# A fused attention and mixture-of-experts layer on one core: where TensorE's products of probabilities and values stand in its queue

## The reference

```python
qkv = x @ w_qkv.T                       # 16 heads of 16
q, k = rope(rms_norm(q)), rope(rms_norm(k))
attn = softmax(causal(q @ k.T) * scale) # per head, 512 x 512
out = (attn @ v) @ w_proj.T
x = layernorm(x + out)
normed = rms_norm(x) * norm_weight
top 2 of 8 experts by sigmoid(normed @ router_w.T), weights normalised
y = relu(normed @ sw1 + sb1) @ sw2 + sb2
  + sum over the chosen experts e: w_e * (relu(normed @ ew1[e] + eb1[e]) @ ew2[e] + eb2[e])
x = layernorm(x + y)
```

## Time and profile before

| | before |
|---|---|
| median of 3 runs | 952.51 us (952.02 to 952.53) |
| profiled execution | 957.52 us, span 955.8 us |
| PE busy | 896.0 us (94%) |
| ACT, DVE, POOL busy | 615.3, 576.6, 457.2 us |
| mean granted TensorE clock | 0.984 |

### The profile page before, as it was taken

The page is one execution under the profiler, slowest core; times in us unless marked ns, Lnnn a source line. Parts: engine busy times, 40 slices in busy tenths (PEclk is TensorE's granted clock), DMA queues, the critical chain, the costliest instruction groups (busy, mean ns, idle before and its releaser), DMA issues.

```text
span 955.8 us, 26112 instructions
## 1 busy us (share of the span) xinstructions
PE 896.0 (94%) x9049; PEld 693.3 (73%) x9050; DVE 576.6 (60%) x1152; ACT 615.3 (64%) x1060; POOL 457.2 (48%) x668
## 2 busy tenths in 40 slices
PE   4789999998999989999999999999999999999995
PEld 1444555555555546888889989989899889898885
DVE  8655698889888636784344444454444433428875
ACT  4788898888878766442656655556655453667753
POOL 5344557877878636572134444344434343412211
PEclk9799999999999989999999999999999999999998
DMA  5112223433212255567882122121212121248641
GB/s 175 67 68 95 94 101 106 158 114 135 101 58 84 69 176 194 202 204 266 267 292 74 50 67 70 52 68 55 67 56 67 46 68 47 74 145 269 214 160 44
DMA packets 68706, 112.76 MB, mean 118 GB/s; under 512 B 7728, under 2 KB 46000, under 8 KB 68496
## 3 DMA queue, kind: packets, MB, share of 16 engines
q1 hardware_dynamic: 51248, 77.32, 24.5%
q10 hardware_dynamic: 10896, 16.40, 5.9%
q0 software_dynamic: 6480, 17.97, 5.2%
HBM read 66.58 MB, written 45.08 MB: 117 GB/s over the span
## 4 chain that ended last, share of the span: by engine, by line
PE 76%; ACT 7%; DVE 6%; issue 4%; POOL 2%; DMA 2%; another core or an unknown queue 1%; ACTq 1%; DVEq 0%; SPq 0%; POOLq 0%
PE hb L1811 23%; PE yb L1827 23%; PE pv_bank L1599 6%; PE slot L1577 4%; PE ma L1612 4%; PE slot L1586 3%; PE hb L1665 3%; ACT prob L872 2%; PE mb L1747 2%; PE ma L1622 1%; PE tr L1685 1%; DMA rs<-resid 1%; PE yb L1702 1%; PE mb L1735 1%
## 5 line engine op out<-in xcount | busy, mean ns | idle before, releaser
L1042 ACT ACTIVATE hf<-hb,b 128x256 f32<-128x256 f32 (+1 forms) x392 | 155.0, 454 | 206.2 <-PE hb L1811 200.7
L1811 PE MATMUL hb<-xgT,wts 128*128 128x256 f16 (+1 forms) x1872 | 213.2, 263 | 1.4 <-ACT hf L1042 1.2
L1827 PE MATMUL yb<-wts,hh 128*128 x1704 | 210.5, 273 | 0.9 <-DVE hh L1454 0.9
L1454 DVE TENSOR_TENSOR hh<-hf,hh 128x1024 f16<-128x1024 f32 (+1 forms) x98 | 120.2, 1229 | 137.3 <-ACT hh L1047 105.4
L1811 PEld LDWEIGHTS hb<-xgT,wts 128*128 x1872 | 181.2, 98 | 20.3 <-ACT hf L1042 1.0
L807 POOL DMA_INDIRECT y_tok<-yb,dest x71 | 77.8, 1096 | 227.0 <-DVE yb L1466 216.9
L1827 PEld LDWEIGHTS yb<-wts,hh 128*128 128x128 f16 x1704 | 166.3, 98 | 19.6 <-DVE hh L1454 1.2
L872 ACT ACTIVATE prob<-slot 128x1024 f32<-128x1024 f32 x160 | 161.6, 1034 | 27.8 <-PE slot L1586 27.3
L1047 ACT ACTIVATE hh<-hf 128x1024 f16<-128x1024 f32 (+1 forms) x98 | 97.6, 996 | 3.1
L741 POOL DMA_INDIRECT xg_rows<-xnh,sl_i x64 | 76.4, 1194 | 16.2 <-issue 13.9
L1577 PE MATMUL slot<-stk 64*128 64x128 f16 (+3 forms) x512 | 64.2, 308 | 16.2 <-ACT prob L872 11.6
(11 more groups left out here) (236 smaller groups left out, 1445.0 us busy)
## 6 DMA issues: line engine op xcount, KB each, us to landing
wts<-in_w_all SPq DMA_DIRECT2D x23, 512.0 KB
wts<-y_tok SPq DMA_DIRECT2D x32, 256.0 KB, 4.9
xg<-xg_rows ACTq DMA_DIRECT2D x30, 264.0 KB
stage<-in_w_all SPq DMA_DIRECT2D x12, 512.0 KB
w_split<-chunk_hl SPq DMA_DIRECT2D x12, 512.0 KB
xTf<-in_xT SPq DMA_DIRECT2D x8, 512.0 KB, 3.8
xin<-in_x SPq DMA_DIRECT2D x8, 512.0 KB
resid<-y SPq DMA_DIRECT2D x16, 256.0 KB
```

The source lines that it names most:

```text
L1042: act.activation(hf[:, c, 0:size], hb[c // 2][:, (c % 2) * TT:(c % 2) * TT + size], ACT.Relu, bias=bias, scale=1.0 / WS).then_inc(S("relu_ ...
L1454: dve.tensor_tensor(hh[:, par, 1, cs, 0:size], hf[:, cs, 0:size], hh[:, par, 0, cs, 0:size], ALU.subtract).then_inc(S("h_lo"), 1)
L1811: ins = pe.matmul(hb[hc // 2][:, (hc % 2) * TT:(hc % 2) * TT + size], weights(e, c, w, hc * P, P), xgT[:, par, x * DC + c, 0:size], start= ...
L1827: ins = pe.matmul(ybank[par][:, j * D:(j + 1) * D], hh[:, par, x, hc, P * j:P * j + P], weights(e, DC + hc * D // CH, w, hc * D % CH, D), ...
```

## The change

PE's call of `attended` is moved within a position from behind the scores to behind RANK, which is behind all jobs but the early shared-expert pieces. The tables of positions, the waits, and the queues of all other engines stay as they are.

```diff
                         scores(c, p)
-                    for c, i in due(AV, g):
-                        attended(c, i)
                     for c, t in due(TR, g):
                         stacked(c, t)
...
                         last.then_inc(S("rank_done"), 1)
+                    for c, i in due(AV, g):
+                        attended(c, i)
                     for kind, m, q in early_due(g):
```

## The result

| | before | changed |
|---|---|---|
| median of 5 runs each | 952.51 us (951.89 to 953.70) | 956.66 us (956.3 to 956.9) |
| ratio | | 1.0053, 95% interval 1.0042 to 1.0064 |
| profiled execution, span | 957.52, 955.8 us | 956.66, 954.9 us |
| mean granted clock | 0.984 | 0.981 |

The change makes the kernel 4.15 us slower, 0.3 us off the forecast of 956.4. One thing in this table needs a word. So the two spans can't be subtracted, and I compare stages that lie ahead of it.

A forecast was written before the change was run, and what follows sets the result against it. PE bounds the kernel, busy 896.0 of 955.8 us. +2.15 us at full clock plus 1.7 us for one clock fall give 3.85 us, so 956.4 us against the median 952.51; range 949.5 to 961.0 us.

The forecast's parts named there:

- Position 6, the waits: TR at position 6 waits for POOL's second copy in batches 3 to 6: some 2.5, 2.5, 1.8, 1.6 us.
- What they cost at full clock: Loss left at position 6 after give-back in batches 3 to 6: 1.2, 1.2, 0 and 0.65 us.
- A place missed: Position 6 of batches 1 and 2: POOL's copies were over before AV began, so no lateness was counted.
- Position 16: ACT's exponential of unit 17 starts sooner: 0.45 us won in batches 0 and 1 each; gains of batches 2 to 5 counted nothing.
- The sum at full clock: Position 16's gains and position 6's losses over all batches: +2.15 us.
- The clock: PE's clock falls to half behind one of the four late places at position 6: 1.7 us.
- the first rival: Serving ACT earlier at position 16 wins, position 6 costs nothing: 2.85 us faster, 949.7 us; chance 0.15.
- The second: Waits at position 6 appear, but the clock holds and some position 16 gain survives: 1.0 us or less, 953.5; chance 0.17.
- The last: Half clock in each late place at position 6: 961.5 us; chance 0.13, shared with a further unseen wait.
- batch 7's gain as 0: NAT passes AV in batch 7, but DVE and ACT would meet the same stall: bounds 0 and -2.2 us, taken 0.

The follow-up runs named there:

- experiment 4: Changed kernel with POOL's scatters of tiles 1 to 3 of batches 0 to 6 moved later, against the kernel before: 954.83 us, ratio 0.9967.
- experiment 2: AV late at position 6 only, at its old place elsewhere, against the kernel before: 959.39 us, ratio 1.0009.
- experiment 1: AV late at position 16 only, at its old place elsewhere, against the kernel before: 954.98 us, ratio 0.9974.
- experiment 9: AV late at position 16 in all batches and at position 6 in batch 7 only, against the kernel before: 950.88 us, ratio 0.9990.
- experiment 10: AV late at position 6 of batches 3 and 4 only, against the kernel before: 955.49 us, ratio 1.0050.
- filled kernel: Changed kernel plus 8 useless fp32 matmuls ahead of TR at position 6, batches 3 to 6, against the kernel before: 956.17 us (0.9975), again 951.43 us (0.9994).
- experiment 5: Changed kernel run again in the second group, against the kernel before: 961.76 us, ratio 1.0046.
- experiment 12: Changed kernel run a third time, in the third group, against the kernel before: 955.81 us, ratio 1.0051.
- experiment 6: Kernel before, unchanged, run again with a profile in the second group: 957.07 us, ratio 0.9994.
- experiment 7: AV late at position 16 only and POOL's scatters late, against the kernel before: 957.56 us, ratio 1.0006.
- experiment 8: Kernel before with POOL's scatters late and nothing else, against the kernel before: 959.25 us, ratio 1.0015.

## Why the prediction was right

By its own steps, in the stage unless said:

- **Position 6, the waits.** Forecast 2.5, 2.5, 1.8, 1.6 us; measured 2.55, 2.63, 1.57, 1.56. Right in place, releaser and size. That POOL's own queue holds the copy is shown by experiment 4.
- **What they cost at full clock.** Forecast 1.2, 1.2, 0 and 0.65; experiment 2 gives 1.09, 1.02, -0.06 and 0.18. Batches 3 to 5 right, batch 6 too high by 0.5: more of the delay was given back than the two waits of PE that I counted. No run singles out where.
- **A place missed.** In batch 2 I called TR free since POOL's copy was over. But TR also waits for `ma_free`, that is for ACT's square of QK, and that costs 0.35 us of waiting. Experiment 2 has +0.40 in that batch; with the gain of position 16 beside it the changed kernel shows -0.17.
- **Position 16.** Batch 0: forecast -0.45. From the start of a score unit at 63.14 us to that of one at 79.05, the stretch that holds position 16, PE takes 15.91 us before and 15.37 in the changed kernel, -0.54. Batch 1: forecast -0.45, and -0.58 in experiment 1 (40.82 to 40.24). I counted the gains of batches 2 to 5 as swallowed. The idle 0.26 and 0.36 us of experiment 1 show the swallowing, but not all of it happens: the changed kernel still has -0.40 in batch 5 against before.
- **The sum at full clock.** Forecast +2.15. Measured: -0.52 ahead of the stage; within it 4.59 - 2 x 1.6 = +1.4; behind it -0.26 (experiment 9). Together +0.6, so this part was too high by some 1.5 us.
- **The clock.** Forecast one fall of 1.7 us, with 0 to 4 possible. The size was right: 1.58 us between experiments 10 and 2, 1.6 between the changed and the filled kernel in both batches (45.23 - 43.60, 46.22 - 44.63), and 1.60 between experiments 5 and 12 in batch 6 (43.28 - 41.68). The number was too low: two in two profiles of the changed kernel, three in the third. This part was too low by 1.5 us. That I took one fall rested on the fall behind the idle 1.96 us at 43 us, and that was one throw of several: the same wait of 1.95 or 1.96 us stands in all 14 profiles and the clock fell behind it in five, and not in the second profile of the kernel before (experiment 6).

So the forecast of +3.85 against +4.15, +4.12 and +3.92 measured is right in mechanism and sign, but its closeness is luck: two errors of 1.5 us and of opposite sign cancel. The terms that were mis-sized are the number of falls, one in place of two or three, and the sum at full clock, +2.15 in place of +0.6.

**The rivals.** The kernel of experiment 1 is what the first rival describes, and its condition, copies that come in time, doesn't hold; so the gain is 1.3 us in the stage, and with batch 0's 0.54 ahead of it some 1.9, and not 2.85. The second, in which the clock holds, is what experiment 2's profile shows, with a stage of +2.63. The last, a half clock in each late place, falls short: behind the waits of 1.56 to 1.58 us the clock held in five of six cases of the changed kernel. The Trainium skill, "TensorE: Matmul & The Clock Gate", section "HAM oscillation — how this bites in real kernels", describes a kernel whose passes each wait for input, longer than PE waits here, and each restart at the low rate. The trace agrees in batches 3 and 4 of all three profiles of the changed kernel and in batch 6 of one, and disagrees in the other five of their twelve late places.

**When does it fall?** Not by the length of the wait alone. It fell behind all six waits of 2.55 to 2.64 us for POOL in the changed kernel, behind 2.26 in experiment 10, and behind 2.51, 2.75 and 1.81 us for an exponential in experiments 4 and 7; it held behind 2.27 and 2.35 in experiment 2, behind 2.35 in experiment 10, and in experiment 8 it held behind one of 2.48 for an exponential; it fell once behind 1.57 (experiment 5). What decides it between 1.6 and 2.5 us is open.

**The stretch at 341 us.** In the first profile of before, ACT and DVE did nothing together for 4.8 us, up to 345.28 us (the prediction saw only its last 2.9). The same in experiment 6, the kernel before in the second group, timelines of ACT and DVE and the busy time:

```profile
345.64 1.02 ACT L872 ACTIVATE prob<-slot 128x1024 f32<-128x1024 f32 x1 [4.79 <-remote]
```

```profile
345.65 0.26 DVE L1190 RECIPROCAL rcp<-mb 128x16 f32<-128x16 f32 x1 [4.70 <-remote]
```

```profile
341.00:346.00 5.00, 2.44 (x32) 1.12 (x22) 0.32 (x2) 0.36 (x1) 2.78 (x3) 0.98 0.32 111
```

The first profile of the changed kernel doesn't have it:

```profile
341.00:346.00 5.00, 4.66 (x54) 2.08 (x54) 4.39 (x10) 2.83 (x4) 3.78 (x5) 1.00 0.42 149
```

It would be easy to credit the change with that. But in all eight profiles of the first two groups ACT idles 4.75 to 5.03 us ahead of one exponential between 342 and 350 us, in those with AV late in batch 7 too, and in all four of the third it idles 2.24 to 2.39 us there, in experiment 10 with AV early in batch 7 too. Between the second AVs of batches 6 and 7 the former take 36.7 to 38.6 us and the latter 33.5 to 33.7. It goes with the group and not with the queue order, nor with the chip, which is the same in the first and third group; and it is of the size by which the medians of before differ, 957.6 to 958.1 against 951.9. Its cause is open. Without the stretch, taking batch 7's gain as 0 was right to 0.2 us. With it batch 7 may well gain: the four profiles with AV late at its position 6 take 36.7 to 38.2 us, three of the four others with the stretch in the groups, and the first profile of before, 38.5 to 38.6, and experiment 1 37.8. The falls of the clock there differ too, so this isn't shown.

**A better version.** AV late at position 16 alone was faster than both kernels in experiment 1, 0.9974; its near twin of experiment 9 gave 0.9990, in an interval that includes 1. The changed kernel with late scatters gave 0.9967. These are gains of 1 to 3 us.

## What to carry to other kernels

Before a job moves behind another one in an in-order queue, look up for each instruction that it will no longer stand in front of when that one's input is made: if the input lands just as the job ends, the job is the cover, and 2.3 us of it become waiting. Earlier results for an engine that isn't the bound pay only as far as the next such place. And where a wait of PE comes near 2.5 us, add the fall of the clock behind it as a term of its own, or give PE something to do there.

## What was not expected of the hardware

- Useless products in a wait make the kernel faster: 4 x 1.9 us of them took 955.81 to 951.43 us; the 2.8 us of it that the profiles show are two falls of the clock that didn't come, less 0.3 us of extra work.
- A fall cost 1.6 us in each of the four comparisons, and the same queue order met two of them or three. The same wait of 1.95 us was followed by a fall in five of 14 profiles.
- One program's profiled execution was 5 us above the median of its timed runs, with a stretch near 341 us in which ACT and DVE stand still together; in every profile of two groups ACT stood still for 4.75 to 5.03 us there and in none of the third.
